# A macaron block: the weights of 9 of 32 expert pairs are loaded during routing, with two x buffers in place of three and a row ring of three in place of four

## The reference

```python
su = x_flat @ w_shared_up                                  # (4096, 256)
shared = silu(g_s) * y_s @ w_shared_down
scores = sigmoid(x_flat @ w_gate)                          # 64 experts
_, topk_idx = top_k(scores, 6)
w = scores_at_topk / their sum
pos = running count of the tokens of each expert;  valid = pos < 256
x_disp = zeros((64, 256, 512)).at[expert, pos].set(x_flat[token])
h_r = silu(x_disp @ w_up[.., 0:64]) * (x_disp @ w_up[.., 64:128])
out_r = h_r @ w_down                                       # (64, 256, 512)
routed = (out_r[expert, pos] * w where valid).sum over the 6 choices
ffn = shared + routed

x = x + 0.5 * ffn(layernorm(x))
x = x + attention(layernorm(x))
x = x + 0.5 * ffn(layernorm(x))
```

## Time and profile before

| what | value |
|---|---|
| median of 3 runs | 3626.76 us (3625.93 to 3632.27) |
| the profiled execution, its own time | 3625.15 us |
| its span | 3623.4 us |
| busy: PE, DVE, ACT, POOL | 86%, 60%, 42%, 55% of the span |
| routing, first and second | 192 and 193 us (3.8 to 195.8 us; 2907.2 to 3100.6 us of the span) |
| experts, first and second | about 427 us each up to POOL's last issue (197.2 to 623.8; 3102.5 to 3530.1) |
| attention with its projections | 633 to 2902 us |
| DMA: bytes, mean rate | 372.48 MB, 103 GB/s |
| mean landing of a weight load in experts (page, 256 KB) | 4.8 to 4.9 us |

### The profile page before, as it was taken

The page is one execution under the profiler, slowest core; times in us unless marked ns, Lnnn a source line. Parts: engine busy times, 40 slices in busy tenths (PEclk is TensorE's granted clock), DMA queues, the critical chain, the costliest instruction groups (busy, mean ns, idle before and its releaser), DMA issues. The chain is left out here.

```text
span 3623.4 us, 52561 instructions
## 1 busy us (share of the span) xinstructions
PE 3098.3 (86%) x16688; PEld 1619.6 (45%) x16688; DVE 2175.9 (60%) x4077; ACT 1516.9 (42%) x2837; POOL 1996.4 (55%) x1137
## 2 busy tenths in 40 slices
PE   7967675698999999999999999999999879667660
PEld 4544443354444444444444444444444346444430
DVE  7923222665778677677777776776777279322222
ACT  3412221232565555555565554655554534222220
POOL 2157776110666566566566665665665611577870
PEclk9978887796999999999999999999999989788885
DMA  6479998743010000100100100101000053699997
GB/s 221 161 201 235 235 234 185 258 178 93 10 30 10 22 30 19 33 10 18 33 18 10 42 11 10 42 11 41 10 10 24 1 178 119 193 236 228 238 198 278
DMA packets 175139, 372.48 MB, mean 103 GB/s; under 512 B 19984, under 2 KB 21008, under 8 KB 174736
## 3 DMA queue, kind: packets, MB, share of 16 engines
q1 hardware_dynamic: 117520, 226.35, 18.8%
q0 software_dynamic: 57344, 142.64, 18.5%
HBM read 222.58 MB, written 154.73 MB: 104 GB/s over the span
## 5 line engine op out<-in xcount | busy, mean ns | idle before, releaser
L1249 POOL TENSOR_TENSOR attention_pair<-attention_prob 128x1024 f32<-128x1024 f32 x512 | 1205.5, 2376 | 825.2 <-ACT attention_prob L1286 825.2
L1453 DVE TENSOR_REDUCE attention_mx<-attention_pM 128x1 f32<-128x512 f32 x2048 | 1266.3, 683 | 322.8 <-PE attention_pM L1350 322.5
L1286 ACT ACTIVATE attention_prob<-attention_pS 128x512 f32<-128x512 f32 x2048 | 1055.3, 606 | 787.4 <-PE attention_pS L1337 784.7
L1337 PE MATMUL attention_pS<-attention_qT,attention_kT 128*128 128x512 f32 x2048 | 857.7, 428 | 23.6 <-ACT attention_prob L1286 14.4
L1350 PE MATMUL attention_pM<-attention_kT,attention_qT 96*128 96x512 f32 x2048 | 840.9, 419 | 10.3 <-DMA attention_qT<-q_parts 10.2
L1337 PEld LDWEIGHTS attention_pS<-attention_qT,attention_kT 128*128 128x128 f32 x2048 | 383.5, 190 | 543.0 <-ACT attention_prob L1286 229.1
L1375 PE MATMUL attention_pO<-attention_prob,attention_v 128*32 128x512 f32 x4096 | 546.4, 605 | 0.0
L624 POOL DMA_INDIRECT sum<-experts_res,c_table x256 | 403.7, 1577 | 123.2 <-issue 83.7
L1350 PEld LDWEIGHTS attention_pM<-attention_kT,attention_qT 96*128 96x128 f32 x2048 | 397.0, 194 | 148.5 <-DVE attention_mx L1453 84.4
L653 PE MATMUL experts_pT<-c_ident,experts_rows 128*128 128x128 f32 x1024 | 203.4, 363 | 255.5 <-DMA experts_rows<-xn_rows,c_table 248.6
L731 DVE COPY experts_xT<-experts_pT 128x512 f32<-128x512 f32 x128 | 88.5, 692 | 544.8 <-PE experts_pT L653 542.7
(11 more groups left out here) (123 smaller groups left out, 2426.0 us busy)
## 6 DMA issues: line engine op xcount, KB each, us to landing
experts_wup<-in_L_ffn_w_up_dram SPq DMA_DIRECT2D x128, 256.0 KB, 4.8
attention_qT<-q_parts SPq DMA_DIRECT2D x96, 256.0 KB, 4.2
xn_rows<-route_xn SPq DMA_DIRECT2D x16, 1152.0 KB, 6.4
sum<-route_sh SPq DMA_DIRECT2D x16, 1024.0 KB, 4.4
experts_wdn<-in_L_ffn_w_down_dram SPq DMA_DIRECT2D x64, 256.0 KB, 4.9
attentionp_got<-sum SPq DMA_DIRECT2D x16, 1024.0 KB, 8.8
combine_got<-sum SPq DMA_DIRECT2D x16, 1024.0 KB, 8.2
route_xt<-in_L_attn_x_dram SPq DMA_DIRECT2D x8, 1024.0 KB, 9.0
```

The lines of the kernel that those rows point to most:

```text
L1249: pool.tensor_tensor(pair[n % 2][:, part], prob[2 * n % PROBS][:, part], prob[(2 * n + 1) % PROBS][:, part], ALU.add).then_inc(s_pair, 1)
L1286: act.activation(prob[t % PROBS][:, h * QT:(h + 1) * QT], pS[:, at, :], ACT.Exp).then_inc(s_ex, 1)
L1337: pe.matmul(pS[:, at, :], kT[:, key:key + P], qT[g][:, h, :], start=True, stop=True).then_inc(s_sc, 1)
L1453: dve.tensor_reduce(mx[:, unit, part:part + 1], pM[:, r % 3, :], X, ALU.max).then_inc(s_mr, 1)
```

## The change

It changes `route`, `experts` and `program`. In both FFNs nine more pairs of weight buffers (`early_weights`) are taken before `route` and given back after `experts`, with a `close` of their own. `route` has two x buffers (`XB` 3 to 2) and three row slots (`RING` 4 to 3). In step i of `route`, behind `load(i + XB)` and the copy, SP issues the weight loads of pair i, in step 0 those of pair 8 too; it waits for all of them once, at the end of the stage. In `experts` pairs 0 to 8 use these buffers, and neither SP nor PE waits for them. SP starts with the loads of pairs 9 and 10 into the two ring buffers, without a wait, and goes on with pairs 11 to 31 under the old waits. No instruction of PE, DVE, ACT or POOL is added, taken away or moved but for the barrier.

```diff
+EARLY_PAIRS = 9
...
+def early_weights(m):
+    return ([m.sb(f"wup{e}", [P, 2, CK, 2 * H]) for e in range(EARLY_PAIRS)],
+            [m.sb(f"wdn{e}", [P, C]) for e in range(EARLY_PAIRS)], m.sem("early"))
...
-    XB, RING, HOTS = 3, 4, 2 * TURN
+    XB, RING, HOTS = 2, 3, 2 * TURN
...
                 for i in range(NTURN):
                     if comes(i + XB):
                         load(i + XB)
...
+                    for e in range(i, EARLY_PAIRS, NTURN):
+                        for a in range(2):
+                            sp.dma_start(wup[e][:, a, :, :], up_view[e, :, a, :, :]).then_inc(s_early, 16)
+                        sp.dma_start(wdn[e][:, :], down_view[e, :, :]).then_inc(s_early, 16)
...
+                sp.wait_ge(s_early, A + 48 * EARLY_PAIRS)
...
-                for e in range(PAIRS):
-                    sp.wait_ge(s_up, A + e - 1)
+                for e in range(EARLY_PAIRS, PAIRS):
+                    if e >= EARLY_PAIRS + 2:
+                        sp.wait_ge(s_up, A + e - 1)
                     for a in range(2):
-                        sp.dma_start(wup[e % 2][:, a, :, :], up_view[e, :, a, :, :]).then_inc(s_w[e % 2], 16)
-                    sp.wait_ge(s_dn[1], A + (e - 1) * HALVES)
-                    sp.dma_start(wdn[e % 2][:, :], down_view[e, :, :]).then_inc(s_wd[e % 2], 16)
+                        sp.dma_start(wup(e)[:, a, :, :], up_view[e, :, a, :, :]).then_inc(s_w[e % 2], 16)
+                    if e >= EARLY_PAIRS + 2:
+                        sp.wait_ge(s_dn[1], A + (e - 1) * HALVES)
+                    sp.dma_start(wdn(e)[:, :], down_view[e, :, :]).then_inc(s_wd[e % 2], 16)
...
+            m = Memory(nc, ffn, "early0")
+            early = early_weights(m)
+            route(nc, "route0", k, gates, x_rows, xn_d, sums[0], True, pairs, early)
+            experts(nc, "experts0", k, pairs, early, xn_d, sums[0])
+            m.close()
```

More of the change, by code:

```diff
@@ L23 @@
 HALVES = CAP // P
+PAIRS = E // 2
+EARLY_PAIRS = 9
 TURN = 4
@@ L112, in setup, with pair_views, route @@
     return k
-def route(nc, tag, k, wts, x_d, xn_d, sums, copy_x):
+def pair_views(w_up, w_down):
+    return (w_up.rearrange("(g a) (p c) h -> g p a c h", a=2, p=P), w_down.rearrange("(g a) h c -> g (a h) c", a=2))
+def early_weights(m):
+    return ([m.sb(f"wup{e}", [P, 2, CK, 2 * H]) for e in range(EARLY_PAIRS)],
+            [m.sb(f"wdn{e}", [P, C]) for e in range(EARLY_PAIRS)], m.sem("early"))
+def route(nc, tag, k, wts, x_d, xn_d, sums, copy_x, pairs, early):
     w_gate, w_su, w_sd = wts
-    XB, RING, HOTS = 3, 4, 2 * TURN
+    XB, RING, HOTS = 2, 3, 2 * TURN
+    up_view, down_view = pairs
+    wup, wdn, s_early = early
     QT = TURN * P
@@ L538, in route, with experts @@
         m.close()
-def experts(nc, tag, k, w_up, w_down, xn_d, sums):
-    PAIRS = E // 2
+def experts(nc, tag, k, pairs, early, xn_d, sums):
     Q = 2 * HALVES
     RING = 4
-    up_view = w_up.rearrange("(g a) (p c) h -> g p a c h", a=2, p=P)
-    down_view = w_down.rearrange("(g a) h c -> g (a h) c", a=2)
+    up_view, down_view = pairs
+    wup_early, wdn_early, _ = early
     with ExitStack() as ctx:
@@ L553, in experts @@
         rows = [m.sb(f"rows{b}", [P, Q, ROW]) for b in range(RING)]
-        wup = [m.sb(f"wup{b}", [P, 2, CK, 2 * H]) for b in range(2)]
-        wdn = [m.sb(f"wdn{b}", [P, C]) for b in range(2)]
+        wup_ring = [m.sb(f"wup{b}", [P, 2, CK, 2 * H]) for b in range(2)]
+        wdn_ring = [m.sb(f"wdn{b}", [P, C]) for b in range(2)]
         xT = [m.sb(f"xT{b}", [P, CK, 2, CAP]) for b in range(2)]
@@ L581, in there, with wup, wdn, loaded @@
             return 0 <= e < PAIRS
+        def wup(e):
+            return wup_early[e] if e < EARLY_PAIRS else wup_ring[e % 2]
+        def wdn(e):
+            return wdn_early[e] if e < EARLY_PAIRS else wdn_ring[e % 2]
+        def loaded(e):
+            return len(range(EARLY_PAIRS + (e - EARLY_PAIRS) % 2, e + 1, 2))
         with nc.Block() as block:
@@ L679, in down @@
                             own = slice(a * H, (a + 1) * H)
-                            pe.matmul(pD[:, h, a, :], hid[b][own, h * P:(h + 1) * P], wdn[b][own, :],
+                            pe.matmul(pD[:, h, a, :], hid[b][own, h * P:(h + 1) * P], wdn(e)[own, :],
                                       start=True, stop=True).then_inc(s_dn[a], 1)
@@ L1542, in program @@
         k = setup(nc, ctx)
-        route(nc, "route0", k, gates, x_rows, xn_d, sums[0], True)
-        experts(nc, "experts0", k, w_up, w_down, xn_d, sums[0])
-        attention(nc, "attention", k, (wq, bq, wk, bk, wv, bv, wo, bo), q_d, sums[0], xb_d, sums[1][0][0:N, :])
-        route(nc, "route1", k, gates, sums[1][0][0:N, :], xn_d, sums[1], False)
-        experts(nc, "experts1", k, w_up, w_down, xn_d, sums[1])
+        pairs = pair_views(w_up, w_down)
+        with ExitStack() as ffn:
+            m = Memory(nc, ffn, "early0")
[3 more added lines that the diff above has]
+            m.close()
+        attention(nc, "attention", k, (wq, bq, wk, bk, wv, bv, wo, bo), q_d, sums[0], xb_d, sums[1][0][0:N, :])
+        with ExitStack() as ffn:
+            m = Memory(nc, ffn, "early1")
+            early = early_weights(m)
+            route(nc, "route1", k, gates, sums[1][0][0:N, :], xn_d, sums[1], False, pairs, early)
+            experts(nc, "experts1", k, pairs, early, xn_d, sums[1])
+            m.close()
         combine(nc, "combine", sums[1], out)
```

16 lines of the change are left out of this document (9 added, 7 removed).

## The result

| what | before | changed |
|---|---|---|
| median of five runs each, measured together | 3626.36 us | 3671.39 us (3667.43 to 3678.18) |
| ratio | | 1.0124, 95% interval 1.0113 to 1.0136 |
| the profiled execution, own time and span | 3625.15, 3623.4 us | 3667.43, 3665.7 us |
| first routing, from its first load of x to `c_table` | 191.6 us | 216.3 us |
| from `c_table` to attention's first load | 438.0 us | 433.9 us |

The change makes the kernel 45.0 us slower. The two routings lose 24.7 and 25.0 us, the two stages of experts give back 4.1 and 2.8, attention 0.7; this is the 42.3 us by which the two profiled spans differ, to 0.2 us.

The account below looks back on a forecast made before the run. DVE was taken to pace routing and POOL's issue list the experts. Terms of +48.2, 0, +3, -4 and +2 gave +49.2 us on 3625.15 us, so 3674 us, 8-in-10 range 3653 to 3693 us.

Parts of the forecast that it names:

- Part 1: Routing: with two x buffers the loads of x come late and DVE waits before `moments`; +48.2 us for both routings.
- Part 2: Routing: with three row slots `normalise` waits for a later row store, which lands 10 us early; cost nothing.
- Part 3: Routing: early weights queued behind the loads of x slow each of ten loads by 0.3 us; +3 us.
- Part 4: Experts: nine pairs without weight loads shrink only POOL's small waits, 2 us a stage; -4 us in all.
- Part 5: End of each FFN's experts: one more close costs 1 us each; +2 us.
- DMA as the bound of the experts: Experts: POOL only follows the DMA engines, so fewer loads save 30.8 us a stage; 3616 us, chance 0.03.
- half absorbed: Routing: loads of x land faster, in 6.6 us, so a late step grows by 2.5 us; 3658 us, chance 0.12.
- weights that fight with the loads: Routing: early weights make each of ten loads of x 1.7 us later; 3688 us, chance 0.13.
- The loads in time: Routing: DVE's stall is hidden, leaving only barriers and the small gain; 3623 us, no change, chance 0.02.

## Why the prediction was right, and where its steps were off

I had forecast 3674 us, between 3653 and 3693; it is 3671.39. The mechanism that carries the sum, the late loads of x, is the one that the runs show. The difference of the profiled executions is 42.3 us where the sum said 49.2: the routings lost 49.7 for 51.2, and the experts with their closes gained 6.9 for 2. Step by step:

**Part 1, two x buffers.** Right in place and nearly in size. Step 0 costs nothing, as costed: 22.27 us and no idle. In step 1 `moments` is 10.87 us late for a predicted 10.1, since the landing took 10.6 and not 9.9 us; the step ends 8.3 us later (65.63 against 57.31) for 7.7. A late step grows by 4.1 us (25.31 against 21.20) and then three times by 3.9, for 4.1. The landing that I took, 8.2 us, came out at 8.1 in the step shown and at 7.8 to 8.5 in the other seven. The output store stood 3.5 us ahead in this step and the next and 4.4 to 5.3 in the others, where I had thought of 5. Put together 8.3 + 4.1 + 3 x 3.9 = 24.1, and the routings lost 24.7 and 25.0. Two x buffers alone made the whole loss in the first set (45.1 us), and the earlier load took it away.

**Part 2, row slots.** Nothing, as costed (ratio 1.0002, and no wait for a slot in the changed kernel).

**Part 3, weights behind the loads.** I took 0.3 us for each of ten loads. The five idles add up to 26.3, 26.2, 28.0 and 26.5 us in the four routings with early weights, and to 25.4, 25.4, 25.1 and 25.6 in the four without: 1.36 us over five loads, 0.27 for each. One routing, that with 28.0, brings a third of it; without it the figure is 0.19. The versions differ in the row slots too, so it is likely, but not shown, that the difference comes from the weights. From the ring order that the Trainium skill states ("DMA: Bandwidth & Descriptors", Queues, rings and completion order) I had concluded 0; the four routings with weights all lie above the four without, so the measurement is weakly against that conclusion. The routings as wholes do not separate: 216.3, 218.1, 220.0 and 219.9 us with the weights, 217.1, 218.0, 217.1 and 215.0 without. The copy of 1 MB, from whose presence I had worked out my upper bound, shows no cost at all: the first routings, which have it, have 25.4 and 25.1, the second ones, without it, 25.4 and 25.6.

**Part 4, nine pairs without loads.** This is the step whose reasoning failed; that its size of -4 comes out near the medians is luck. I said that only POOL's small waits could shrink, 2 us a stage, and that "the first add keeps its 11.85 us". In the profiled executions the stages became 5.0 and 3.6 us shorter from the first gather to the last add's issue. But with two x buffers alone, where nothing in the experts is changed, they were shorter by 7.4 and 5.3 in one execution and by 6.0 and 5.0 in the other. The small waits of the kernel before (10.3 and 11.4 us a stage without the first add) are 4.2 to 6.4 us in those, and 4.0 to 5.8 in the versions with three row slots or an additional close alone; in the changed kernel they are 6.7 and 9.0 us in the first profile and 3.6 and 7.0 in the second. They come and go between executions of like kernels, and the one execution from which I had read them had the most of all that load each weight once, so they were no term to divide by 30 pairs. In the first 140 us of its first stage, where the early pairs are, the kernel before had 0.95 us of them; that is all there was to win. The first add came 2.0 and 1.7 us sooner in the first profile of the changed kernel, but not in the second (29.46 and 29.57 us after the first gather); in the first, PE's first products ran at the upper level of the clock. What can be won is the first add's wait, which I had set as fixed. It goes from 12.15 to 7.7 us once no weight load runs beside the first gathers, and the whole kernel is then 14.4 us faster than before in the medians. The change leaves 1.5 MB just there. With the loads of x in time, nine early pairs were worth 3.3 us, and six with their closes 4.3, hardly more than the noise. Beside the late loads no gain could be told: the changed kernel is 45.0 us above the kernel before and two x buffers alone 45.1, and in the last set 49.8 and 46.3, where parts 3 to 5 of the sum say that the change is 1 us above the two buffers.

**Part 5, the closes.** Predicted +2; 1.3 us in the medians, which is within the noise, and 0.5 to 0.6 us each over all profiles.

**The rivals.** DMA as the bound of the experts (3616 us) is refuted by both directions: taking all weight loads out of the experts gave 17.2 us, where at 230 GB/s the 32 pairs, 25.2 MB, would be 109 us a stage, and adding two thirds again cost 11.5 us, where it would have been 73 us a stage. The two that came nearest, half absorbed (3658) and weights that fight with the loads (3688), fail on the idles of 3.8 us and on 0.27 us a load. The loads in time (3623) is what the earlier load makes of the same buffers.

**What stays open.** I did not settle what decides whether the clock of the first products is at its upper or lower level. With 1.5 MB of loads beside the gathers, where PE was idle for 12.0 to 13.4 us before the first transposes, both levels occur. Without them, with PE idle for 10.4 to 10.6 us, five of six stages had the upper one. The sixth is the second stage of the version with two early pairs: the clock was 0.53, the 32 products took 5.96 us, and the first add came 24.81 us after the first gather in place of 22.73 in the first stage. The idle before was nearly the same (10.64 us in the first stage, 10.35 in the second), so it doesn't decide alone. Why the small waits differ between executions was not tried either, nor why routing and attention were longer in the slowest execution of the changed kernel.

## What to carry to other kernels

When a buffer is given up, look at the place of the load in its issuer's list before the size of the load: each load now serves a reader one turn sooner, and the whole cost here was one position in SP's list, which moving the call took back. Prefetching pays where the consumer stands idle, which for these weights was only the start of a stage: two pairs loaded ahead and the others held back until the first gathers are through gave more (12 us) than six or nine pairs ahead with the others let go at once (3 to 4). Before a waiting time of one execution is made a term of a sum, see whether it is in other executions of like kernels.

## What the runs showed of the hardware that I had not expected

The gathers at the start of a stage feel 1.5 MB of loads that are issued 0.5 us ahead of them: PE's first transposes begin 9.4 to 10.7 us after the first gather's start with these loads, and 7.7 to 8.0 without. With the doubled up weights, 2.5 MB at this place, it is 11.3 and 11.4. The idle of PE ahead of them, in the version with all nine pairs and the loads held back:

```profile
205.20 3.89 PE L687 MATMUL experts_pT<-c_ident,experts_rows 128*128 128x128 f32 x16 [10.58 <-DMA experts_rows<-xn_rows,c_table]
```

It is 13.39 us in the row with the loads above.

A DMA share near 1 meant little: it read 0.94, 0.99, 1.01 and 1.05 for 175, 235, 239 and 278 GB/s in the same 260 us, with POOL's pace the same within 2% (162 to 165 instructions).

The length of POOL's issue of an indirect DMA did not depend on the weight loads. The adds' mean is 1576 or 1577 ns before, in the changed kernel, with no weight loads and with doubled ones.
